# Two expert layers of a four-layer kernel: the base stored ahead of the rows, gate weights gathered apart from the rows, and half an expert's weights split per chunk in the first layer

## The chip, the cores and the metric

The kernel runs on one NeuronCore of one Trainium2 chip. The metric is the device time of one execution in microseconds; lower is better. The kernel before takes 2632.61 us, the median of 3 runs (2631.84 to 2633.73). The profile comes from one further execution, which took 2637.3 us.

The engines are called by their profile names where rows are quoted: PE (TensorE), DVE (VectorE), ACT (ScalarE), POOL (GpSimd) and SP (SyncE, which here only issues DMAs).

## The reference

The input `x` is (4, 512, 256), so T = 2048 tokens of D = 256 values, beside a context of 4 x 1601 rows. Four layers are added to `x` in turn, each fed with a layer norm of `x`:

```python
x = x + L0_xattn(ctx, layernorm(x))    # 8 heads of 128, keys from the context and x
x = x + L0_ffn(layernorm(x))           # experts, layer 0 below
x = x + L1_xattn(ctx, layernorm(x))    # 8 heads of 32
x = x + L1_ffn(layernorm(x))           # experts, layer 1 below
```

The two expert layers are what the change touches. Each has 8 experts with weights (256, 1024) and (1024, 256).

- Layer 0: scores = softmax(xn @ w_router); each token goes to its best two experts; an expert takes the first 512 of its tokens and drops the rest; h = gelu_tanh(rows @ w1); y = h @ w2; the output of a token is the sum of its score times y, plus a bias.
- Layer 1: the two largest logits (with a bias) get a softmax among themselves; h = gelu(x @ W1 + b1) with the exact gelu; out is the weighted sum of h @ W2 + b2; nothing is dropped.

## The kernel before, in words

`X` holds the 2048 tokens in SBUF as 16 tiles of 128. The function `experts` (from L940) is called once per expert layer, with `layer` 0 or 1. It has an opening and a loop over chunks of 256 rows.

**Precision.** A float32 operand is represented by two float16 numbers, a high one and a low one, and a product takes three matmuls. Expert weights come from HBM as float32 into the tile `stage` (two halves, w1 and w2, 1 MB each). `split_high` on ACT (L1176) writes the high part of a quarter of a half, `split_low` on DVE (L1183) the low part. An expert has PIECES = 8 such quarters; both functions count on semaphores (`s_wh`, `s_wl`), and SP loads a half of the next expert when the low parts of that half of the last one are written (`load_weights`, L1260).

**The opening.** PE transposes `X` and computes logits; DVE takes the statistics of the layer norm; POOL computes 1/sqrt; ACT writes the normalized rows into `xn` in two halves of eight tiles (`normalize`, L1417), splits expert 0's first half (four pieces), computes the exponential `ex` (L1435) and goes on splitting. DVE chooses the two experts of each token, and writes the gate weights `wst` (L1684, L1686). PE sums ranks (L1505 to L1511), DVE turns them into slot positions and builds one-hot matrices in `xn`'s space (L1710 to L1716), which must wait until the rows have left `xn` for HBM (L1708). PE multiplies the one-hots into the list of tokens per slot (L1535), and DVE makes `gidx` and `sidx` of it, the row indices for gathering and for scattering. In layer 1, PE also multiplies the gate weights with b2 (`pe_weighted_bias`, L1512): four before the one-hot products and four after them; ACT copies the results into `wb`.

**DMAs of the opening.** SP's queue, in order: small constants, expert 0's weights, the rows `xn` into the HBM tensor `xrow` (four parts, and in layer 1 a fifth), the gate weights into the last 8 of the 264 columns of `xrow`, expert 1's weights, then the base: `X` into the sums tensor `yd` (L1287, L1288; called `f_sums` in the rows). POOL gathers the rows of chunks 0 and 1 by an indirect DMA of 128 rows each, two per chunk, with the gate weights in the same row of 264 values (L1368 to L1372). Then it waits for the base and adds the bias (layer 0) or `wb` (layer 1) to it by four accumulating DMAs (L1393).

**The loop.** Layer 0 has 16 chunks, two per expert; layer 1 has 23, and a table that names each chunk's expert. A chunk n is turned (`pe_turn`: four transposes into `psX`; `act_turn` and `dve_turn` copy the high and low parts into `xh` and `xl`), and its 1024 hidden values are computed in 8 tiles f: `pe_hidden`, a GELU on ACT twice (L1204 to float16, L1206 to float32), the low part on DVE (L1235), `pe_output`. The turn of chunk n+1 stands inside chunk n, at f = 3 (PE) and f = 4 (ACT, DVE), and its first two hidden tiles are computed at the end of chunk n. In a chunk of the splitting loop, ACT and DVE split one piece of expert n + EARLY = n + 2 behind each f, so a whole expert's weights per chunk, until all 8 are there (`LOOPS`, L1245: three pairs of chunks with splits, the others without). In the opening, experts 0 and 1 are split, and chunk 0's first product waits until all of expert 0 is (L1545). At a chunk's end DVE multiplies the output by the gate (L1741), and POOL scatters it into the sums with two indirect accumulating DMAs (L1376). POOL's order for chunk n: gather chunk n + 2, wait for DVE, scatter chunk n. The first scatter also waits until the bias transfers have landed. The layer is over when the last scatter has landed.

## Time and profile before

| | us |
|---|---|
| median of 3 runs | 2632.61 |
| the profiled execution | 2637.3 |
| its span | 2635.5 |
| PE busy | 2417.4 (92%) |
| DVE busy | 1903.0 (72%) |
| POOL busy | 1725.7 (65%) |
| ACT busy | 1675.6 (64%) |

All stages are in one timeline, counted from the span's start. Layer 0 of the experts starts at about 1466 and ends at about 1725; layer 1 starts at about 2288 and goes to the end. A "granted clock" of 1.0 is 2.4 GHz for PE, 0.5 is 1.2 GHz. In a row of a timeline the number in brackets is the engine's idle time just before the instruction, and what ended it. Busy time of an engine counts no waiting; what an engine waits for shows in the brackets only.

### The profile page before, as it was taken

The numbers are of one execution on the slowest core, as the hardware profiler recorded it, in microseconds if no ns is written. First come the engines' busy times: TensorE is split into PE (matmuls) and PEld (weight loads), VectorE is DVE, ScalarE is ACT, GpSimd is POOL, SyncE is SP. The second block draws the span as 40 slices with busy tenths as digits, with TensorE's granted clock in tenths as the row PEclk, the third lists the DMA queues.
The fourth block names the chain that finished last, engine by engine and source line by source line (L and its number), as shares of the span: only waits on it lengthen the run. The fifth ranks groups of instructions, "written<-read, shape, count | busy, mean of one in ns | idle before, by whom it ended". The sixth has DMA issues, their size and how long they took to land. (4 is left out here: it accounts for less than half of the span.)

```text
span 2635.5 us, 45921 instructions
## 1 busy us (share of the span) xinstructions
PE 2417.4 (92%) x14931; PEld 1421.2 (54%) x15058; DVE 1903.0 (72%) x3499; ACT 1675.6 (64%) x2694; POOL 1725.7 (65%) x1503
## 2 busy tenths in 40 slices
PE   6999999999999999999998379969999999779997
PEld 3455555555555455555554268834444444458886
DVE  7878777787777877777777565448888889767443
ACT  4556756557655566655655366427888888758664
POOL 2687878687877777767678335417777779724443
PEclk9999999999999999999999589979999999869999
DMA  4000000000000000000000384241211010175323
GB/s 146 1 1 1 26 1 1 1 1 1 26 1 1 1 1 1 1 1 1 1 1 1 97 251 94 41 113 40 53 27 48 23 38 14 50 219 154 49 45 65
DMA packets 88425, 107.89 MB, mean 41 GB/s; under 512 B 16371, under 2 KB 77764, under 8 KB 88212
## 3 DMA queue, kind: packets, MB, share of 16 engines
q1 hardware_dynamic: 68500, 80.57, 10.1%
q0 software_dynamic: 19200, 24.97, 5.8%
q8 instruction: 107, 1.75, 0.3%
q14 instruction: 74, 0.60, 0.1%
q10 hardware_dynamic: 544, 0.00, 0.0%
HBM read 68.75 MB, written 25.88 MB: 36 GB/s over the span
## 5 line engine op out<-in xcount | busy, mean ns | idle before, releaser
L425 POOL TENSOR_TENSOR a_acc<-a_acc,a_pf 128x512 f32<-128x512 f32 (+1 forms) x480 | 655.3, 1365 | 309.4 <-ACT a_pf L582 287.7
L582 ACT ACTIVATE a_pf<-a_psS 128x1024 f32<-128x1024 f32 (+1 forms) x288 | 281.2, 976 | 306.4 <-PE a_psS L725 300.4
L2082 POOL TENSOR_TENSOR c_pl<-c_pf,c_ph 128x512 f16<-128x512 f32 x320 | 375.2, 1201 | 124.4 <-ACT c_ph L2181 124.0
L877 DVE TENSOR_TENSOR a_pl<-a_pf,a_ph 128x512 f16<-128x512 f32 x448 | 435.1, 981 | 23.4 <-ACT a_ph L588 23.3
L853 DVE TENSOR_REDUCE a_mx<-a_psA 128x1 f32<-128x512 f32 x504 | 337.2, 684 | 45.9 <-PE a_psA L660 40.8
L1376 POOL DMA_INDIRECT f_sums<-f_xn,f_sidx x78 | 138.0, 1770 | 235.3 <-DVE f_xn L1741 199.4
L588 ACT ACTIVATE a_ph<-a_psS 128x1024 f16<-128x1024 f32 (+1 forms) x288 | 281.0, 976 | 0.0
L2413 DVE TENSOR_REDUCE c_mx<-c_psA 128x1 f32<-128x512 f32 x384 | 246.8, 683 | 20.4 <-PE c_psA L2252 20.2
L2174 ACT ACTIVATE c_pf<-c_psS 128x1024 f32<-128x1024 f32 x192 | 197.5, 1029 | 68.9 <-PE c_psS L2286 67.6
L1235 DVE TENSOR_TENSOR f_xn<-f_xn 128x256 f16<-128x256 f32 x312 | 129.9, 424 | 134.8 <-ACT f_xn L1206 130.5
L848 DVE TENSOR_TENSOR a_vl<-a_psA,a_vh 128x256 f16<-128x256 f32 (+1 forms) x266 | 112.5, 423 | 140.8 <-ACT a_vh L511 138.1
L747 PE MATMUL a_psO<-a_pl,a_vh 128*128 128x512 f16 (+1 forms) x544 | 206.1, 379 | 7.2 <-POOL a_pl L443 7.2
L741 PE MATMUL a_psO<-a_ph,a_vh 128*128 128x512 f16 (+1 forms) x544 | 206.1, 379 | 4.0 <-DVE a_ol L882 3.9
L601 PE MATMUL a_psS<-a_qh,a_kh 128*128 128x512 f16 (+1 forms) x544 | 206.2, 379 | 0.2
L603 PE MATMUL a_psS<-a_qh,a_kl 128*128 128x512 f16 (+1 forms) x544 | 206.2, 379 | 0.0
L602 PE MATMUL a_psS<-a_ql,a_kh 128*128 128x512 f16 (+1 forms) x544 | 206.2, 379 | 0.0
L742 PE MATMUL a_psO<-a_ph,a_vl 128*128 128x512 f16 (+1 forms) x544 | 206.0, 379 | 0.0
L2181 ACT ACTIVATE c_ph<-c_psS 128x1024 f16<-128x1024 f32 x192 | 197.3, 1028 | 0.0
L660 PE MATMUL a_psA<-a_kh,a_qh 128*128 128x512 f16 x504 | 191.5, 380 | 4.2 <-DVE a_mx L853 0.4
L1135 PE MATMUL f_psH<-f_xh,f_w 128*128 128x256 f16 x624 | 172.9, 277 | 24.3 <-ACT f_xn L1206 12.7
L842 DVE SCALAR_TENSOR_TENSOR a_kl<-a_psA,a_bkv,a_kh 128x512 f16<-128x512 f32 (+1 forms) x156 | 102.8, 659 | 115.4 <-ACT a_kh L505 115.3
L1136 PE MATMUL f_psH<-f_xl,f_w 128*128 128x256 f16 x624 | 172.4, 276 | 0.0
(354 smaller groups left out, 6309.9 us busy)
## 6 DMA issues: line engine op xcount, KB each, us to landing
f_stage<-in_L_ffn_w SPq DMA_DIRECT2D x16, 1024.0 KB
f_stage<-in_L_ffn_W SPq DMA_DIRECT2D x16, 1024.0 KB, 5.6
c_kst<-c_khs SPq DMA_DIRECT2D x64, 100.1 KB, 2.2
a_cx<-in_ctx SPq DMA_DIRECT2D x4, 1536.0 KB
c_cx<-in_ctx SPq DMA_DIRECT2D x12, 512.0 KB, 3.9
f_xrow<-f_xn SPq DMA_DIRECT2D x8, 512.0 KB, 3.0
f_sums<-X SPq DMA_DIRECT2D x2, 2048.0 KB, 12.5
c_kst<-c_kls SPq DMA_DIRECT2D x32, 100.1 KB, 2.2
```

The lines of the kernel that those rows point to most:

```text
L425: g.tensor_tensor(acc[0:k, p, :], acc[0:k, p, :], pf[0:k, q % RF, i, :], ALU.add).then_inc(s_acc, 1)
L582: act.activation(pf[0:r, q % RF, 0:k, :], psS[q % 2][0:r, 0:k, :], ACT.Exp, scale=SCALE).then_inc(s_pF, 1)
L588: act.activation(ph[0:r, q % RP, 0:k, :], psS[q % 2][0:r, 0:k, :], ACT.Exp, scale=SCALE).then_inc(s_pH, 1)
L601: pe.matmul(out, hi, xh_, start=first, stop=False)
L602: pe.matmul(out, hi, xl_, start=False, stop=False)
L603: return pe.matmul(out, lo, xh_, start=False, stop=last)
L741: pe.matmul(psO[:, :], vh[0:r, g % 2, j, vs], ph[0:r, q % RP, i, :], start=(j == 0), stop=False)
L747: ins = pe.matmul(psO[:, :], vh[0:r, g % 2, j, vs], pl[0:r, q % RP, i, :], start=False, stop=(j == JT0 - 1))
L853: v.tensor_reduce(mx[:, n % 2, it, c:c + 1], ps[:, 0:KCH[c][1]], AX.X, ALU.max).then_inc(s_fr, 1)
L877: v.tensor_tensor(pl[0:r, q % RP, i, :], pf[0:r, q % RF, i, :], ph[0:r, q % RP, i, :], ALU.subtract).then_inc(s_pL, 1)
L2082: g.tensor_tensor(pl[0:r, q % RP, i, :], pf[0:r, q % RF, i, :], ph[0:r, q % RP, i, :], ALU.subtract).then_inc(s_pG, 1)
L2413: ins = v.tensor_reduce(mx[:, n % 2, it, c:c + 1], ps[:, 0:KCH[c][1]], AX.X, ALU.max)
```

## The change

Both layers:

- SP stores the base `X` into `yd` ahead of the rows and not behind expert 1's weights.
- Rows and gate weights lie in two HBM tensors, `xrow` (256 columns) and `wrow` (8 columns). POOL gathers each chunk's rows with two indirect DMAs and its weights with two more, counted on a semaphore pair of their own, `s_xw`. DVE's `dve_gate` waits for it. The store of the gate weights no longer waits for the row stores.
- ACT performs a GELU on one column, `warm`, ahead of the first turn.
- PE's first product waits for the first half of expert 0's pieces alone.

Layer 0 alone: the exponential stands between the two halves of `normalize`; POOL adds the bias to the base ahead of the first gather; expert 0's pieces have their low parts made behind the indices, all eight; expert 1 is not split in the opening. In the loop, chunk p of pair m splits half p of expert m + 1, one piece at each even f, and there is one loop over seven pairs with splits.

Layer 1 alone: one more weighted bias (of the four behind) is put between the one-hot products; the first half of expert 1 is split between the weighted biases (ACT) and behind the table (DVE), the second half behind the first turn.

The diff, cut to its core:

```diff
@@ expert weights and gate
-        s_xb, s_ys, s_bst = pool_sems
+        s_xb, s_ys, s_bst, s_xw = pool_sems
...
             for f in range(2, FT):
                 pe_hidden(pe, L, n, p, e, f)
+                if f == 2 and splits and not layer and p == 0:
+                    pe.wait_ge(s_wl, (m + 2) * PIECES)
                 pe_output(pe, L, n, p, e, f - 2)
...
-            if splits:
+            if splits and layer:
                 pe.wait_ge(s_wl, (n + 3) * PIECES)
+            elif splits and p == 1:
+                pe.wait_ge(s_wl, (m + 2) * PIECES + PH)
...
+        def split_at(m, p, f):
+            if layer:
+                return [(m * 2 + p + 2, f)]
+            return [(m + 1, p * PH + f // 2)] if f % 2 == 0 else []
...
-                if splits:
-                    split_high(act, n + EARLY, f)
+                for e, q in split_at(m, p, f) if splits else ():
+                    split_high(act, e, q)
...
-        def dve_gate(v, p, e):
+        def dve_gate(v, m, p, e):
+            v.wait_ge(s_xw[p], m * 16 * IT + 16 * IT)
+            v.nop(nofuse=True)
...
-        LOOPS = ((0, (E - EARLY) // 2, True), ((E - EARLY) // 2, PAIRS, False))
+        LOOPS = ((0, (E - 2) // 2, True), ((E - 2) // 2, PAIRS, False)) if layer else ((0, PAIRS, True),)
@@ block.sync
             for half in range(2):
                 load_weights(0, half)
+            sp.dma_start(yd[0:T, :]..., X[:, :, :]).then_inc(s_base, 16)
+            sp.dma_start(yd[T:T + CH, :]..., X[:, 0:IT, :]).then_inc(s_base, 16)
...
             sp.wait_ge(s_wst, 1)
-            sp.wait_ge(s_xst, 16 * (NQ + layer))
-            sp.dma_start(xrow[0:T, D:ROW]..., wst[:, :, :]).then_inc(s_wd, 16)
+            sp.dma_start(wrow[0:T, :]..., wst[:, :, :]).then_inc(s_wd, 16)
...
             for half in range(2):
                 load_weights(1, half)
-            sp.dma_start(yd[0:T, :]..., X[:, :, :]).then_inc(s_base, 16)
-            sp.dma_start(yd[T:T + CH, :]..., X[:, 0:IT, :]).then_inc(s_base, 16)
@@ block.gpsimd
+            def gather_weights(n):
+                for u in range(IT):
+                    g.indirect_dma_start(xb[:, n % 2, u, D:ROW], None, wrow, rows_in(n, u)).then_inc(s_xw[n % 2], 16)
...
+            if not layer:
+                g.wait_ge(s_small, 16 * NSMALL)
+                add_base(lambda q: bias[:, :].unsqueeze(1).broadcast_to([P, 4, D]))
             g.wait_ge(s_xst, 16 * (NQ + layer))
-            g.wait_ge(s_wd, 16 * (1 + layer))
             g.wait_ge(s_gidx, 1)
             gather(0)
+            g.wait_ge(s_wd, 16 * (1 + layer))
+            gather_weights(0)
             gather(1)
+            gather_weights(1)
+            if layer:
+                g.wait_ge(s_wbF, NT // 2)
+                add_base(lambda q: wb[:, 4 * q:4 * q + 4, :])
             for n in range(NC):
                 if n + 2 < NC:
...
                     gather(n + 2)
+                    gather_weights(n + 2)
@@ block.scalar
             normalize(0)
+            if not layer:
+                exponentials()
             normalize(1)
...
+                    if i == NB2 - 1:
+                        for q in range(PH):
+                            split_high(act, 1, q)
+            act.wait_ge(s_const, 3)
+            act.activation(warm[:, :], onef[:, :], GELU)
             act_turn(act, main, 0, 0)
+            if layer:
+                for q in range(PH, PIECES):
+                    split_high(act, 1, q)
@@ block.tensor
             for i in range(2 * NT):
+                if layer and i == 2 * NT - 2 * NT // NLO:
+                    pe_weighted_bias(NB2)
...
-            pe.wait_ge(s_wl, 2 * PIECES)
+            pe.wait_ge(s_wl, PIECES + PH)
             for f in range(2):
                 pe_hidden(pe, main, 0, 0, 0, f)
+            if layer:
+                pe.wait_ge(s_tab, 1)
+                pe.wait_ge(s_wl, 2 * PIECES)
@@ block.vector
-            for q in range(PH):
-                split_low(v, 0, q)
+            if layer:
+                for q in range(PH):
+                    split_low(v, 0, q)
...
-            for q in range(PH, PIECES):
+            for q in range(PH if layer else 0, PIECES):
                 split_low(v, 0, q)
...
-            for q in range(PIECES):
-                split_low(v, 1, q)
+                for q in range(PH):
+                    split_low(v, 1, q)
             dve_turn(v, main, 0, 0)
             if layer:
                 dve_bias(v, main, 0, 0, 0, wait=False)
+                for q in range(PH, PIECES):
+                    split_low(v, 1, q)
```

## Rows read from the trace of the kernel before

**Rows 1.** Busy time by stage; columns as its second line says, clock, DMA share, GB/s

```profile
1521.00:1563.00 42.00, 33.91 (x254) 26.36 (x255) 24.32 (x50) 26.54 (x66) 16.12 (x12) 0.83 0.93 246
1610.00:1725.00 115.00, 104.86 (x945) 90.54 (x943) 46.29 (x114) 53.70 (x160) 50.35 (x36) 0.99 0.28 43
```

**Rows 2.** Waits, 1520 to 1730: us in total, times, longest

```profile
POOL f_sums L1376 <- DVE f_xn L1741: 81.0, 15, 7.5
```

**Rows 3.** Timeline of the turns on ACT, layer 0: start, us, instruction

```profile
1531.24 0.66 ACT L1191 ACTIVATE f_xh<-f_psX 128x512 f16<-128x512 f32 x1
1550.07 0.60 ACT L1191 ACTIVATE f_xh<-f_psX 128x512 f16<-128x512 f32 x1
1563.02 0.60 ACT L1191 ACTIVATE f_xh<-f_psX 128x512 f16<-128x512 f32 x1
...
1610.11 0.60 ACT L1191 ACTIVATE f_xh<-f_psX 128x512 f16<-128x512 f32 x1
...
1701.80 0.60 ACT L1191 ACTIVATE f_xh<-f_psX 128x512 f16<-128x512 f32 x1
```

**Rows 4.** Timeline of the opening of layer 0, ACT and DVE

```profile
1478.09 7.95 ACT L1421 ACTIVATE f_xn<-X,f_shift,f_rstd 128x256 f32<-128x256 f32 x16
...
1488.35 0.29 DVE L1667 TENSOR_REDUCE f_sm<-f_ex 128x16 f32<-128x128 f32 x1 [5.21 <-ACT f_ex L1435]
...
1493.20 2.49 DVE L1187 SCALAR_TENSOR_TENSOR f_w<-f_stage,f_w 128x512 f16<-128x512 f32 x4
...
1498.03 1.29 DVE L1710 TENSOR_TENSOR f_xn<-f_ihi,f_hi 128x512 f16<-128x512 f16 x2
```

**Rows 5.** Windows of 2 us: us, POOL busy, PE clock, DMA share, GB/s

```profile
1522.00:1524.00 2.00, 0.00 (x0) 0.50 1.10 405
...
1530.00:1532.00 2.00, 1.39 (x3) 1.00 1.24 200
```

**Rows 6.** Timeline, chunk 0's gather and turn in layer 0

```profile
1510.52 1.22 POOL L1370 DMA_INDIRECT f_xb<-f_xrow,f_gidx  x1 [0.30 <-issue]
...
1517.55 1.11 PE L1124 MATMUL f_psX<-identf,f_xb 128*128 128x128 f32 x4 [9.82 <-DMA f_xb<-f_xrow,f_gidx]
...
1519.86 0.57 ACT L1191 ACTIVATE f_xh<-f_psX 128x512 f16<-128x512 f32 x1
```

**Rows 7.** Instruction groups, both layers: busy us, mean ns, idle before

```profile
L1204 ACT ACT_TABLE_LOAD x6 | 7.7, 1283 | 5.6 <-PE f_psH L1137 5.4
```

**Rows 8.** Timeline, waits in chunks 0 and 1 of layer 0

```profile
1527.03 0.63 ACT L1181 ACTIVATE f_w<-f_stage 128x512 f32 x1 [1.92 <-DMA f_stage<-in_L_ffn_w]
...
1541.37 0.63 ACT L1181 ACTIVATE f_w<-f_stage 128x512 f32 x1 [4.92 <-DMA f_stage<-in_L_ffn_w]
...
1547.01 1.11 PE L1124 MATMUL f_psX<-identf,f_xb 128*128 128x128 f32 x4 [3.13 <-DMA f_xb<-f_xrow,f_gidx]
```

**Rows 9.** The gathers of line 1370: ns min/median/max, first and last start

```profile
L1370 POOL DMA_INDIRECT f_xb<-f_xrow,f_gidx x78: 949/1018/1489, 1508.9 to 2592.5; - x78
```

**Rows 10.** Timeline of layer 1's opening and first chunks, PE, POOL and ACT

```profile
2326.81 7.19 PE L1516 MATMUL f_psH<-f_b,f_wt 8*128 8x256 f32 x16
...
2329.62 1.35 POOL L1370 DMA_INDIRECT f_xb<-f_xrow,f_gidx  x1 [0.30 <-ACT f_w L1445]
...
2337.19 1.09 PE L1124 MATMUL f_psX<-identf,f_xb 128*128 128x128 f32 x4 [3.19 <-DMA f_xb<-f_xrow,f_gidx]
...
2339.34 0.57 ACT L1191 ACTIVATE f_xh<-f_psX 128x512 f16<-128x512 f32 x1
...
2351.57 0.64 ACT L1191 ACTIVATE f_xh<-f_psX 128x512 f16<-128x512 f32 x1
...
2360.94 0.63 ACT L1181 ACTIVATE f_w<-f_stage 128x512 f32 x1 [3.74 <-DMA f_stage<-in_L_ffn_W]
...
2367.56 0.60 ACT L1191 ACTIVATE f_xh<-f_psX 128x512 f16<-128x512 f32 x1
...
2380.54 0.64 ACT L1191 ACTIVATE f_xh<-f_psX 128x512 f16<-128x512 f32 x1
```

More of the change, by code:

```diff
@@ L959, in experts @@
     HR = ring(FT, 3)
-    PIECES, EARLY = FT, 2
+    PIECES = FT
     PH = PIECES // 2
@@ L1732, in _ @@
                 v.sem_inc(s_tab, 1)
-            for q in range(PIECES):
-                split_low(v, 1, q)
+                for q in range(PH):
+                    split_low(v, 1, q)
             def take_rows(m, p):
@@ L2485, in build @@
                       [ctx.enter_context(nc.semaphore(f"f{l}_ys{p}")) for p in range(2)],
-                      ctx.enter_context(nc.semaphore(f"f{l}_bst"))) for l in range(2)]
+                      ctx.enter_context(nc.semaphore(f"f{l}_bst")),
+                      [ctx.enter_context(nc.semaphore(f"f{l}_xw{p}")) for p in range(2)]) for l in range(2)]
         sums = [nc.dram_tensor(f"f{l}_sums", (B * S + 2 * P, D), F32, kind="Internal").ap() for l in range(2)]
```

62 lines of the change are left out of this document (29 added, 33 removed).

## The prediction, made before the changed kernel ran

> **What bounds the kernel now.** I read the page first: the slices show TensorE at nine tenths nearly everywhere and low in two places, the openings of the two expert layers. The table of stages comes next [rows 1]: in the opening chunks of layer 0 (1521 to 1563) TensorE is busy 33.9 of 42 us at a mean granted clock of 0.83 while the DMA engines are 0.93 busy; in that layer's undisturbed part (1610 to 1725) the clock is 0.99 and the DMA engines 0.28 busy. There the table of waits [rows 2] shows GpSimd waiting for VectorE before each scatter, 81.0 us in 15 times, so 5.4 us a chunk: GpSimd has room. The timeline of the turns (the copy of a chunk's transposed rows to `xh`, one per chunk) gives the pace [rows 3]: from 1610.11 to 1701.80 eight chunks take 11.46 us each, and this is TensorE's own pace. Before it, the turn of chunk 2 comes 18.83 us after that of chunk 1, the next 12.95 us later, and the four after 47.09 us together. So a layer is a fixed pace behind a serial opening, and what the opening or its first chunks lose is lost in the end: the scatter of the last chunk ends each layer.
>
> **The change, part by part, layer 0.** *Softmax ahead.* VectorE waits 5.21 us for the exponential, until 1488.35, so its logits were ready at 1483.14; ScalarE has it behind all 16 normalizations (7.95 us from 1478.09) and four weight pieces [rows 4]. Now it stands behind eight normalizations, done at 1478.09 + 4.0 = 1482.1, so it starts at about 1483.3: VectorE resumes 4.75 us earlier. *Four low splits out of the chain.* 2.49 us of VectorE [rows 4] leave the stretch between the gate weights and the slot positions; part of them covered TensorE's rank products, so I count 1 us. The one-hots, from 1498.03, could start at 1492.3. *Base stored first.* They also wait until the normalized rows have left `xn`. The 2.36 MB of base now go into the row stores' queue in front of them. At the 405 GB/s of [rows 5] they need 5.8 us, begin when the first weights are in (about 1475.6) and are out by about 1482. The accumulating bias transfer follows at once, where the DMA engines are 1.24 busy and move only 200 GB/s [rows 5], so it takes some 10 to 12 us, from about 1484, beside the second half of the row stores (1.6 us per 512 KB alone, twice that when shared), the last of which is now issued at 1487.5, since the exponential and the later normalizations move it by 1.4 us. I put their landing at 1494.5: the one-hots gain 3.5 us, not 5.7. Bounds: no sharing, 5.7; the rows behind the whole accumulation (about 1500), a loss of 2. *Gather.* The second half of chunk 0's rows is issued by 1511.74 and TensorE starts on them at 1517.55 [rows 6], 5.8 us later, with a weight load and the base beside them. Now the base is gone and the weight loads start after the gather. Bounds: 5.8 again, or 2 us. I take 3.0, near the low end because the gather's neighbours leave: gain 2.8. *Splits behind the turn.* Four weight pieces on ScalarE kept the turn at 1519.86 [rows 6], though the four transposes ended 1.11 us after 1517.55: 1.2 us gained, since expert 1 is not split in the opening any more. Opening: 3.5 + 2.8 + 1.2 = 7.5 us.
>
> The Trainium skill ("DMA: Bandwidth & Descriptors", Anatomy of one DMA) fits a software-made DMA as 2.0 us plus bytes over 436e3, so 2.3 us for half a chunk's rows; by that estimate the gather would gain 3.5 us instead of my 2.8, and the measured 5.8 us is what crowded engines make of it.
>
> *First chunks of layer 0.* Six table loads of 1.283 us each stand before a GELU [rows 7]: in both layers at the first GELU and at the head of the first loop's two later rounds. The `warm` GELU makes one of each three, hidden in the wait for the gather, and leaves the loop none: the second loop, which is entered from a GELU, shows none today. ScalarE also waits 1.92 us for a stage in chunk 0 and 4.92 us in chunk 1, and TensorE 3.13 us for the rows of chunk 2 [rows 8]. Both have one cause, the crowd on the DMA engines: base, bias and weights two experts ahead, all after 1511. In the new kernel base and bias are done at about 1497, chunk 0 needs only the first half of expert 1, and chunk 1 the second. So chunk 2's turn comes 11.46 us after chunk 1's instead of 18.83: 7.4 us (the fallen clock after the stall is in this number). The next gains 12.95 - 11.46 = 1.5. The four to 1610.11 lose 47.09 - 45.84 = 1.25, a table load and a change of loops; I take 1.0. Chunk 0's own first interval, 11.38 us, holds a table load and the 1.92; TensorE's work at half clock stands right behind them, so of 3.2 I take 2.0. *Half an expert a chunk.* 56 splits in the loop instead of 48, four a chunk to the last pair. The chunks with eight splits keep the pace apart from those 1.25 us, and ScalarE has 53.7 of 115 us busy in the unsplit part [rows 1], so four (2.5 us) are nearly free; I charge 0.1 us for each of eight more chunks, 0.8. Layer 0: 7.5 + 2.0 + 7.4 + 1.5 + 1.0 - 0.8 = 18.6 us.
>
> *Weights gathered apart*, both layers. Two more indirect DMAs a chunk on GpSimd. No row has a gather of 32 bytes a row; the nearest is the row gather, median 1.02 us [rows 9] and 0.30 us to the next instruction, so 2.6 us a chunk, out of 5.4 us of waiting [rows 2]: nothing. In the opening they push gather(1) back by 2.6 us, needed only at the fourth tile of chunk 0, about 7 us after the first turn. VectorE's new wait for them stands behind the low half of the turn, and ahead of the first `hl`, 4 us later; they land before. Bounds: nothing, and with 5 us a pair the excess over the cover, which is a rival below.
>
> **Layer 1.** *One weighted bias between one-hot products.* Four of them take 7.19 us [rows 10], one 1.8. It goes into a gap of 0.7 us, in which TensorE waits for the last one-hots, so the slot indices come 1.1 us later. *Gather and turn.* Issued by 2330.97, rows used at 2337.19 [rows 10], 6.2 us later; with the base gone but a weight load beside it I take 4.1 (bounds 2 and 6.2): 2.1 gained. The turn at 2339.34 waited behind four splits, psX being ready at 2338.28: 1.0. So 2.0 in all. *First chunks.* Interval of the turns 12.23 us, then 15.99, then 12.98 [rows 10]. The first has a table load and a wait for a stage, as in layer 0: 2.0 gained. The second holds ScalarE's 3.74 us wait for a stage [rows 10] and one for rows. Here the accumulation cannot start before the weighted biases and four more gathers (about 2340, 4 us earlier than now), and expert weights still go two ahead: the crowd is only thinned by the base's 6 us. Bounds 0 and 4.3; I take the middle, 2.4. The third gains most of its table load, 0.8, and a later one 0.4. Layer 1: 2.0 + 2.0 + 2.4 + 0.8 + 0.4 = 7.6 us. Base before the row stores costs nothing there: weights, base and rows are 6.8 MB, 17 us at 405 GB/s from the stage's start at about 2291, so out by some 2312 with the gaps; the one-hots that wait for them are built in the ten us before 2326.81.
>
> **Sum.** 18.6 + 7.6 = 26.2 us. The profiled execution has 2637.3 us (span 2635.5 and 1.8 around it) and gives 2611.1; the median, 2632.6, gives 2606.4. I forecast 2606.5.
>
> ScalarE's page of the Trainium skill ("ScalarE: Activation LUTs", What ACT_TABLE_LOAD costs) adds a drain of about 1.38 us to each load, so 2.66 us. Six loads, two of them left and hidden, would by that return up to 16 us in place of the 5 or so that I have for them in the terms above. The rows do not bear it out: four chunks with one load and a change of loops in them lose 1.25 us in all against the pace [rows 3].
>
> **Rivals.** *A, the row stores are caught behind the accumulation* in layer 0. For it: both start within a few us, and accumulation halves the rate [rows 5]. Against: the stores of three quarters are issued before it is under way. Where the rows land only at 1500, the 3.5 turn into -2: 2606.5 + 5.5 = 2612. *B, layer 1 gains only its opening and tables*, since its crowd is merely moved: without 2.4 and half of the first interval's 2.0, 2606.5 + 3.4 = 2610; with the gathers of both layers no faster (2.8 + 2.1) it is 2615. For it: [rows 10] show weights late with hardly any base left in the queue. *C, the openings clear out completely*: no sharing of the row stores (2.2), layer 1's second interval at its best (1.9), gathers at 2 us (1.0 + 2.1): 2606.5 - 7.2 = 2599. *D, GpSimd becomes the bound*: two weight gathers a chunk cost more than the 5.4 us of cover. It decides from 2.7 us for each. At 3.5 us each, seen nowhere in the trace (longest gather 1.49 [rows 9]), it is 1.6 us over in each of 37 chunks, 59 us, less the 26 gained: 2640, slower. *E, the change does not do what it says*: table loads stay in the loops because the compiler places them anew; 3 us less gain, 2609.5.
>
> **How the numbers follow.** Forecast 0.45, A 0.15, B 0.17, C 0.13, D 0.03, E 0.07. The range takes in C and both forms of B: 2599 to 2617. What a measurement can tell from no change is 0.2%, 5.3 us. Faster than that: all but D and a rest in which several bad ends meet, 0.95; within it 0.02; slower 0.03.
>
> **What would show it.** The exponential of layer 0 at about 1483 and one-hots from 1492 to 1497, with VectorE waiting for the row stores if I am right on sharing; turns of chunk 0 near 1512 and 2337; three turns in layer 0 at 11.5 us from the second on, without a clock at half; one table load a layer, ahead of the first turn; GpSimd's wait before scatters at 2.7 us. The forecast is wrong if a chunk's pace in the later part of either layer moves by more than 0.2 us (rival D or dearer splits), if one-hots start after 1498, or if layer 1 still has a 16 us interval.

## The result, and the profile after

| | before | after |
|---|---|---|
| median, us | 2632.23 (2631.44 to 2633.73, 4 runs) | 2617.27 (2615.52 to 2619.40, 4 runs) |
| the profiled execution, us | 2637.3 | 2615.5 |

The ratio is 0.9944, 95% interval 0.993 to 0.9959: 15 us faster, where 26 were forecast. A later comparison on another chip (`after_control` below) has 0.9955 (0.9941 to 0.9968), 10.6 us. The time lies just outside the range, above its upper end of 2617.

Layer 0's opening is where the forecast and the chip part first. The timelines of ScalarE, VectorE, GpSimd, SyncE and TensorE in the kernel after (columns as in [rows 3] and [rows 4]):

```profile
1483.44 0.31 ACT L1455 ACTIVATE f_ex<-f_sh 128x128 f32<-128x128 f32 x1 [1.12 <-DVEq L1702]
...
1492.20 0.19 DVE L1749 TENSOR_TENSOR f_hi<-f_pos,f_lo 128x32 f16<-128x32 f32 x1
1499.94 1.29 DVE L1752 TENSOR_TENSOR f_xn<-f_ihi,f_hi 128x512 f16<-128x512 f16 x2 [7.55 <-DMA f_xrow<-f_xn]
...
1483.36 5.52 POOL L1396 DMA_DIRECT2D f_sums<-f_bias  x4 [2.89 <-DMA f_sums<-X]
1510.72 1.26 POOL L1387 DMA_INDIRECT f_xb<-f_xrow,f_gidx  x1 [21.84 <-DVE f_gidx L1760]
1512.29 1.38 POOL L1387 DMA_INDIRECT f_xb<-f_xrow,f_gidx  x1 [0.30 <-issue]
...
1480.38 7.68 SPq L1294 DMA_DIRECT2D f_xrow<-f_xn  x4
1512.83 2.78 SPq L1284 DMA_DIRECT2D f_stage<-in_L_ffn_w  x2
...
1518.11 1.11 PE L1126 MATMUL f_psX<-identf,f_xb 128*128 128x128 f32 x4 [8.49 <-DMA f_xb<-f_xrow,f_gidx]
```

The exponential stands at 1483.44, as forecast, and VectorE has the slot positions at 1492.39. Then it waits 7.55 us for the row stores out of `xn`: the one-hots start at 1499.94, 1.9 us after those of [rows 4], and not 3.5 us before. SyncE issues the four row stores at 1480.38, 1482.35, 1485.74 and 1487.70; GpSimd issues the four accumulations of the bias from 1483.36 to 1488.88, so three of them go out ahead of the third row store. The last row store, from issue to landing, in the kernel after, and then in `e1_again` (below), where no accumulation runs beside it (count, KB, us to landing):

```profile
f_xrow<-f_xn SPq DMA_DIRECT2D x1, 512.0 KB, 12.1
```

```profile
f_xrow<-f_xn SPq DMA_DIRECT2D x1, 512.0 KB, 3.1
```

The windows of that stretch in the kernel after (POOL busy, clock, DMA share, GB/s):

```profile
1486.00:1488.00 2.00, 2.00 (x3) 0.50 1.09 151
...
1492.00:1494.00 2.00, 0.00 (x0) 0.50 1.20 210
...
1496.00:1498.00 2.00, 0.00 (x0) 0.50 1.24 226
1498.00:1500.00 2.00, 0.00 (x0) 0.50 1.46 201
1500.00:1502.00 2.00, 0.00 (x0) 0.50 0.88 85
```

The packets' times add up to more than the 16 engines have (a share over 1), and in these windows the engines move 151 to 226 GB/s, near the 200 GB/s of the accumulation in [rows 5], until about 1501. The last accumulation has landed at 1502.7. The turns of layer 0 after that, and two turns from its later part:

```profile
1528.58 0.60 ACT L1204 ACTIVATE f_xh<-f_psX 128x512 f16<-128x512 f32 x1
1539.88 0.60 ACT L1204 ACTIVATE f_xh<-f_psX 128x512 f16<-128x512 f32 x1
1551.66 0.60 ACT L1204 ACTIVATE f_xh<-f_psX 128x512 f16<-128x512 f32 x1
...
1608.99 0.60 ACT L1204 ACTIVATE f_xh<-f_psX 128x512 f16<-128x512 f32 x1
...
1689.21 0.60 ACT L1204 ACTIVATE f_xh<-f_psX 128x512 f16<-128x512 f32 x1
```

The first turn is at 1519.26 (before: 1519.86), and then 9.32 and 11.30 us follow where [rows 3, 6] had 11.38 and 18.83. The windows that answer [rows 1], and GpSimd's wait that answers [rows 2]:

```profile
1519.00:1561.00 42.00, 39.68 (x338) 33.49 (x337) 24.82 (x55) 27.16 (x74) 23.82 (x20) 0.93 0.48 126
...
POOL f_sums L1401 <- DVE f_xn L1783: 47.5, 16, 8.9
```

TensorE has 39.7 of 42 us busy (33.9 before), the DMA engines 0.48 (0.93). GpSimd's wait ahead of the scatters is 47.5 us in 16, 3 us a chunk, and still a wait: the two weight gathers a chunk, 0.94 us each, are covered. The pace is unmoved: 11.46 us a chunk from 1608.99 to 1689.21 (seven chunks), as in [rows 3].

Layer 1's turns, GpSimd's stretch behind them, and TensorE's wait for chunk 2's rows:

```profile
2320.98 0.60 ACT L1204 ACTIVATE f_xh<-f_psX 128x512 f16<-128x512 f32 x1 [2.57 <-PE f_psX L1126]
2330.68 0.60 ACT L1204 ACTIVATE f_xh<-f_psX 128x512 f16<-128x512 f32 x1
2347.51 0.60 ACT L1204 ACTIVATE f_xh<-f_psX 128x512 f16<-128x512 f32 x1
2360.20 0.60 ACT L1204 ACTIVATE f_xh<-f_psX 128x512 f16<-128x512 f32 x1
...
2322.86 5.38 POOL L1396 DMA_DIRECT2D f_sums<-f_w  x4
2328.54 1.11 POOL L1387 DMA_INDIRECT f_xb<-f_xrow,f_gidx  x1 [0.30 <-issue]
2344.39 1.71 POOL L1401 DMA_INDIRECT f_sums<-f_xn,f_sidx  x1 [10.57 <-DMA f_sums<-f_w]
...
2345.35 0.65 PE L1126 MATMUL f_psX<-identf,f_xb 128*128 128x128 f32 x4 [2.52 <-DMA f_xb<-f_xrow,f_gidx]
```

The second interval, chunk 1's, is 16.83 us, against 15.99 in [rows 10] and 13.6 forecast.

A stage that the change doesn't touch also moved: from the last turn of layer 0 to layer 1's exponential it is 607.2 us before and 603.1 after. The windows of that attention stage, before and after (columns as in [rows 1]):

```profile
1725.05:2288.62 563.57, 518.35 (x2716) 258.51 (x2716) 465.76 (x823) 435.79 (x516) 405.30 (x367) 0.96 0.16 41
```

```profile
1712.46:2271.59 559.13, 512.74 (x2716) 256.71 (x2716) 465.02 (x823) 435.65 (x516) 405.04 (x367) 0.98 0.16 41
```

The same 2716 products, granted 0.96 and 0.98. Over all 21 traces this stretch, from turn to exponential, lies between 602.9 and 608.1 us with no relation to the edits, so its 4.1 us (4.4 between the edges of these windows) are not put down to the change. Stages are therefore compared below from marks inside them.

### The profile page after: what moved, and what is told of

The parts are those of the page before. It is cut to its first block and busy times, and to the rows that moved or that the text cites. A ratio compares the mean times of both kernels' runs of the same rounds, so it can differ in the third digit from the quotient of the medians.

```text
span 2613.7 us, 46134 instructions
## 1 busy us (share of the span) xinstructions
PE 2408.0 (92%) x14931; PEld 1418.7 (54%) x15058; DVE 1906.1 (73%) x3499; ACT 1673.0 (64%) x2692; POOL 1806.8 (69%) x1581
## 5 line engine op out<-in xcount | busy, mean ns | idle before, releaser
L877 DVE TENSOR_TENSOR a_pl<-a_pf,a_ph 128x512 f16<-128x512 f32 x448 | 437.1, 985 | 23.4 <-ACT a_ph L588 23.3
L2457 DVE TENSOR_REDUCE c_mx<-c_psA 128x1 f32<-128x512 f32 x384 | 246.7, 683 | 19.9 <-PE c_psA L2296 19.7
```

What stands on the lines that cost most here:

```text
L877: v.tensor_tensor(pl[0:r, q % RP, i, :], pf[0:r, q % RF, i, :], ph[0:r, q % RP, i, :], ALU.subtract).then_inc(s_pL, 1)
L2457: ins = v.tensor_reduce(mx[:, n % 2, it, c:c + 1], ps[:, 0:KCH[c][1]], AX.X, ALU.max)
```

## The experiments

Marks: N is the start of layer 0's normalization, X the exponential of layer 1, T0, T1, ... the turns (in the text N to T0 means the time between them). All columns are us; "time" is the median of the kernel's runs (one run where it stands in brackets), "pace" is one chunk between T8 and T15 of layer 0. Six of them ran at a slower pace, as the last column shows (see below).

| kernel | time | N to one-hots | N to T0 | T0 to T2, layer 0 | X to T0 | T0 to T2, layer 1 | pace |
|---|---|---|---|---|---|---|---|
| before | 2632.2 | 19.9 | 41.8 | 30.2 | 30.3 | 28.2 | 11.5 |
| c1_before_again | 2629.1 | 19.9 | 41.9 | 30.2 | 30.2 | 27.9 | 11.4 |
| after | 2617.3 | 21.6 | 41.0 | 20.6 | 28.7 | 26.5 | 11.5 |
| after_control | 2618.7 | 20.9 | 40.3 | 21.0 | 29.0 | 26.7 | 11.5 |
| c0_after_again | 2682.9 | 21.6 | 41.1 | 20.2 | 29.1 | 26.1 | 13.4 |
| e1_bias_after_rows | 2674.0 | 14.4 | 31.5 | 22.6 | 28.8 | 26.3 | 13.8 |
| e1_again | 2608.7 | 14.3 | 31.5 | 20.1 | 28.9 | 26.6 | 11.5 |
| e1_third | 2607.4 | 14.4 | 31.5 | 20.3 | 28.9 | 26.5 | 11.5 |
| e2_stage_held | (2621.0) | 20.7 | 37.5 | 21.2 | 28.9 | 27.8 | 11.5 |
| v2 | 2609.3 | 14.3 | 30.5 | 21.2 | 28.9 | 27.4 | 11.5 |
| e5_no_warm_gelu | (2615.2) | 20.7 | 40.3 | 20.3 | 28.9 | 26.2 | 11.5 |
| e6_base_back | (2697.5) | 14.1 | 33.6 | 31.6 | 29.6 | 29.2 | 13.9 |
| e6_again | (2626.4) | 14.1 | 33.5 | 31.8 | 29.5 | 29.4 | 11.5 |
| e8 | (2620.4) | 20.4 | 39.8 | 26.0 | 28.7 | 26.0 | 11.4 |
| e9 | (2619.9) | 21.2 | 40.5 | 21.3 | 28.1 | 27.5 | 11.5 |
| e3_gather2_first | (2691.6) | 20.9 | 40.6 | 20.7 | 29.0 | 24.0 | 13.5 |
| e4_l1_no_accum | (2684.9) | 22.0 | 41.4 | 20.7 | 28.9 | 23.3 | 13.8 |
| e4_again | (2612.3) | 20.5 | 39.9 | 21.0 | 28.9 | 22.1 | 11.5 |
| v1 | 2690.1 | 24.0 | 43.4 | 21.1 | 33.4 | 28.5 | 13.7 |
| v3 | 2606.1 | 14.4 | 31.2 | 20.8 | 26.0 | 25.3 | 11.5 |

The kernels whose opening of layer 0 is that of the kernel after have one-hots 20.4 to 22.0 us behind N: a difference under 2 us there says little, and against the 19.9 of before they lose 0.5 to 2.1.

**The bias accumulated behind the rows (e1).** Rival A, put to the test:

```diff
-            if not layer:
-                g.wait_ge(s_small, 16 * NSMALL)
-                add_base(...bias...)
             g.wait_ge(s_xst, 16 * (NQ + layer))
+            if not layer:
+                g.wait_ge(s_small, 16 * NSMALL)
+                add_base(...bias...)
```

> The changed kernel with one move in layer 0: the accumulating bias transfers are issued only when the row stores have landed. Main theory: the one-hots of layer 0 waited 7.55 us for the rows (until 1499.94) because the accumulation ran beside the row stores. Then they start at 1492.5 to 1494 here, the turn of chunk 0 moves from 1519.3 to 1512 to 1514, and the time falls by 5.5 to 7 us (about 2611). Rival: the rows are late because they stand behind the 2.36 MB of base in the same queue. Then the one-hots start no earlier than 1498 and the time stays within 2 us.

The one-hots start 14.4 us behind N and the first turn 31.5, 9.5 us earlier than in the kernel after, so the theory held and its 5.5 to 7 us were too few. The base still stands in front of the row stores here, which rules out the rival. The total went the other way, 2674.04 us (2672.93 to 2678.09), because its loops ran at another pace; see the control below. Repeated beside a copy of the kernel after:

> Layer 0's four accumulations of the bias are issued behind the wait for the rows' stores, and not in front of them. In one look their one-hot matrices started 14.35 us behind the start of the normalization against 21.6 in the kernel after, and the first turn came 31.5 us behind it against 41.0; the third turn 8.3 to 9.1 us earlier. Theory: 8 to 9 us faster than the kernel after beside it, and 2607 to 2610 where that takes 2617: the forecast gain of layer 0's opening was to be had. Rival: the accumulations, now landing beside the first gather, cost it again in chunks 0 to 2, and it gains 0 to 4 us.

Measured 2608.68 (2604.73 to 2611.27, 5 runs), ratio to before 0.9918 (0.9904 to 0.9931), against 2618.70 (2614.43 to 2619.19) for `after_control`: 10 us faster by moving one wait over four DMAs. The opening of `e1_again`:

```profile
1491.05 5.53 POOL L1396 DMA_DIRECT2D f_sums<-f_bias  x4 [10.65 <-DMA f_xrow<-f_xn]
1502.78 1.11 POOL L1387 DMA_INDIRECT f_xb<-f_xrow,f_gidx  x1 [6.20 <-DVE f_gidx L1760]
...
1492.57 1.29 DVE L1752 TENSOR_TENSOR f_xn<-f_ihi,f_hi 128x512 f16<-128x512 f16 x2
...
1509.73 0.60 ACT L1204 ACTIVATE f_xh<-f_psX 128x512 f16<-128x512 f32 x1 [16.46 <-PE f_psX L1126]
1518.56 0.60 ACT L1204 ACTIVATE f_xh<-f_psX 128x512 f16<-128x512 f32 x1
```

The row stores have landed by 1491.05, VectorE waits for nothing, and the accumulation runs while VectorE builds the one-hots. Against `after_control` the accumulation in front costs 6.6 us of one-hots and 8.8 of the first turn; from N to the last turn of layer 0 it is 201.0 us for 210.7.

**Two paces of one program.** On the chip of the first e1 ran also e3, e4 and e6. e3 moves layer 1's accumulation behind chunk 2's gather:

```diff
-            if layer: ... add_base(...wb...)
             for n in range(NC):
                 if n + 2 < NC: ... gather(n + 2); gather_weights(n + 2)
+                if layer and n == 0: ... add_base(...wb...)
```

> The changed kernel with one move in layer 1: the gathers of chunk 2 are issued ahead of the accumulating transfers. Theory a: the 16.8 us interval of the turns of chunks 1 and 2 has 2.5 us of waiting for rows because the gather stands in GpSimd's queue behind the accumulation (plus the fall of the clock, if any, after it). Then the interval is 13.5 to 14.5 us. Theory b: it is the bandwidth that the accumulation takes, whatever the order. Then the gather's wait shrinks little, or comes back one chunk later, since the first scatter waits for the accumulation: the sum of the two intervals (29.5 us) stays within 1 us.

e4 leaves that accumulation out, so its output lacks the term with b2:

```diff
                 g.wait_ge(s_wbF, NT // 2)
-                add_base(lambda q: wb[:, 4 * q:4 * q + 4, :])
+                g.wait_ge(s_base, 32)
...
-                    g.wait_ge(s_bst, 16 * NQ)
+                    if not layer:
+                        g.wait_ge(s_bst, 16 * NQ)
```

> The changed kernel without the accumulating transfers of layer 1 (the weighted bias b2 is left out of the sums; all else is computed). Theory a (the accumulation is what crowds chunk 1): the intervals of the turns, 16.8 and 12.7 us, become 11.5 to 12.3 and 11.7; layer 1 loses 5 to 6 us. Theory b (expert weights two experts ahead are enough of a crowd by themselves): ScalarE's waits for a stage, 2.1 and 0.9 us in chunks 0 and 1, remain and the first interval stays above 13.5 us.

e6 puts the base's stores back, and with them layer 0's bias accumulations behind the gathers of chunks 0 and 1 (the diff shows the first part):

```diff
-            sp.dma_start(yd[0:T, :]..., X[:, :, :]).then_inc(s_base, 16)
-            sp.dma_start(yd[T:T + CH, :]..., X[:, 0:IT, :]).then_inc(s_base, 16)
...
             for half in range(2):
                 load_weights(1, half)
+            sp.dma_start(yd[0:T, :]..., X[:, :, :]).then_inc(s_base, 16)
+            sp.dma_start(yd[T:T + CH, :]..., X[:, 0:IT, :]).then_inc(s_base, 16)
```

> The changed kernel with the base stored behind expert 1's weights again, and layer 0's bias added behind the gathers of chunks 0 and 1, as before; the rest of the change stays. Main theory: layer 0's one-hots no longer wait for the rows (start 1492.5 to 1493.5, gain 7 us), but the crowd of base, bias and weights is back in the first chunks: the gather lands 1 to 2 us later than in the changed kernel, and chunks 1 and 2 lose 3 to 8 us; in layer 1 the interval of chunks 1 and 2 stays at 16 us or more. Rival: with half an expert a chunk the crowd no longer matters in layer 0, and the intervals stay at 11.3 to 11.8 us: then this version is faster than the changed kernel by 6 us or more.

And the kernel after, with no edit:

> The changed kernel, unchanged, run again beside the others. Four variants of it, whose PE instructions are the same, took 2674 to 2697 us, with a pace of 13.7 us a chunk in layer 0 where the changed kernel had 11.5, and PE 'issue' waits of 20 us in a stretch of 100. If the slow pace belongs to the variants' own edits, this one repeats 2617 us. If it belongs to a property of the program's loading or of the run (where the loop's instructions lie, how they are fetched), this one may show 2670 us or more too, though nothing in it differs.

All six programs on these two chips (v1 below is the sixth) took 2674 to 2697 us, and `c0_after_again`, which is the kernel after to the last instruction, 2682.87 (2681.77 to 2683.97). The kernel before, beside them, kept its time (2631.96 and 2633.24). Its loop, ScalarE from 1610 and the weight loads' waits from 1600 to 1700 (us in total, times, longest), then the same waits in the first trace of the kernel after:

```profile
1612.29 0.41 ACT L1219 ACTIVATE f_xn<-f_psH 128x256 f32<-128x256 f32 x1
1614.83 0.38 ACT L1217 ACTIVATE f_xn<-f_psH 128x256 f16<-128x256 f32 x1 [2.13 <-PE f_psH L1139]
...
PEld f_psH L1137 <- issue: 19.7, 19, 2.0
```

```profile
PEld f_psH L1137 <- issue: 2.3, 4, 0.7
```

Engines stop in turn for 1 to 2 us behind nothing that the profile shows. It isn't TensorE's clock: the window of 1600 to 1700 (PE busy, clock, DMA share, GB/s) of `c0_after_again`, then of the kernel after, has the clock at 1.00 in both and the DMA engines equally busy.

```profile
1600.00:1700.00 100.00, 85.47 (x748) 1.00 0.48 113
```

```profile
1600.00:1700.00 100.00, 97.61 (x876) 1.00 0.47 106
```

Layer 0 takes 27 us more from its first to its last turn (197.3 for 170.4), layer 1 36 more from X to its last turn (324.7 for 289.0). The marks ahead of the loops differ far less: those of `c0_after_again` lie within 0.8 us of `after_control`, those of the first e4 within 1.6 us of `e4_again`, and T0 to T2 of the first e1 (22.6) is 2.5 us off. So the openings can be read, for effects well above that.

> The kernel before, unchanged, placed beside itself as the other experiments are, since the kernel after took 2683 us so placed against 2617 when it was first measured, with its expert loops at 13.7 us a chunk against 11.5. Theory 1: any program placed as the experiments are pays this in its expert loops; then this copy takes about 2690 to 2700 us against 2632 of the same instructions beside it, with turns of layer 0 in the loop 13 to 14.7 us apart instead of 11.3 to 12.1. Theory 2: only the change's loops can fall into the slower pace; then it takes 2632 and its turns stand 11.3 and 12.1 apart.

2629.06 (2626.93 to 2631.14), beside 2629.46 for the kernel before: unmoved. But this doesn't decide between the theories, since the kernels beside it, and all that ran later on two more chips, had the normal pace, among them e1, e4, e6 and the kernel after, unchanged:

> The kernel after, unchanged, as the control beside the next three. On two chips a copy took 2683 us with its expert loops at 13.7 us a chunk; on the chip of the first measurement 2617, and three near-copies on another chip took 2615, 2620 and 2621. If the slower pace belongs to some chips or loads, this copy and its three neighbours stand at the same pace, whichever it is; if it belongs to single programs, they differ from each other.

Kernels of the new form on one chip agreed each time, so the pace goes with the chip or the occasion and not with the edit, and the kernel before has never shown it. What it is stays open.

**The stage loads held (e2, v2).** SyncE waits for chunk 0's rows before it loads expert 1:

```diff
+            if not layer:
+                sp.wait_ge(main.xb[0], 16 * IT)
             for half in range(2):
                 load_weights(1, half)
```

> SyncE's two stage loads of expert 1 in layer 0 (1 MB each) wait until chunk 0's rows are gathered. In the kernel after, the gather's second issue ended at 1513.67 and TensorE's first transpose of its rows started at 1518.11: 4.4 us where 3.0 were predicted; the stage loads are issued from 1512.83 and fill all queues from 1515. Theory (the gather's packets stand behind the stage loads'): without them the gather lands 2.5 to 3.2 us after its issue, the first turn is 1.2 to 1.9 us earlier, and chunk 0's splits of expert 1 start 3 to 4 us later, so that the third turn gains nothing. Rival (the landing is the gather's own): 4.4 us as before, the first turn unmoved and the next two later. The total isn't decisive at this size; the turns are.

The second gather issue ended at 1513.23 and TensorE had the rows 1.8 us later:

```profile
1515.07 1.11 PE L1126 MATMUL f_psX<-identf,f_xb 128*128 128x128 f32 x4 [5.89 <-DMA f_xb<-f_xrow,f_gidx]
```

1.8 for 4.4 us: the loads had stood in the gather's way. The first turn comes 2.9 us earlier (1.2 to 1.9 expected) and the third 2.7, 58.7 us behind N for 61.4 in `after_control`, where no gain was expected. No gain shows in the total of the one run, 2620.98, with 2 us of it in the untouched stage and 2.6 more in layer 1.

> As e1_again, and SyncE's two stage loads of expert 1 in layer 0 wait until chunk 0's rows are gathered. The hold by itself brought the first turn 3.0 us forward and the third 2.4 us; in the one look at the later bias the gather landed 2.85 us behind its issue without a hold, against 4.4. Theory 1 (both waits are of the same queue, and the later bias has already moved the stage loads off the gather): as e1_again within 1 us, or up to 1 us slower, since the stage loads come later. Theory 2 (they add up): 2 to 3 us faster than e1_again.

2609.28 (2604.69 to 2611.49), as e1: theory 1. The gather landed in 1.85 us against 2.86, and the first turn is 1.0 us earlier, which the next interval gives back, 9.9 for 8.8. TensorE's mean granted clock in that interval is 0.70 for 0.74; over the kernels at the normal pace (the kernel before and e8 apart) it is 8.8 to 10.1 us long, so a difference of 1 us there is not put down to an edit.

**The table loads (e5).**

```diff
-            act.wait_ge(s_const, 3)
-            act.activation(warm[:, :], onef[:, :], GELU)
```

> Leaves out ScalarE's warm-up activation behind the softmax, so the table load for the activation function falls behind the first turn again, in both layers. Theory of the prediction (a table load of 1.28 us is on the path only if it stands behind the turn): the first turn of either layer is unmoved within 0.3 us, and the interval from the first to the second turn grows by 1.0 to 1.3 us in each layer against the kernel after placed alike (9.76 and 9.29 us there). Rival: ScalarE waits there for the hidden products anyway (the wait of 2.4 us ahead of the first of them), and the intervals stay.

2615.24, and intervals of 8.99 and 9.89 us where `after_control` has 9.74 and 10.10. The loads are back:

```profile
L1217 ACT ACT_TABLE_LOAD x10 | 12.8, 1283 | 6.5 <-PE f_psH L1139 6.4
```

Ten for two, and nothing lost in one run (2615.24 lies within the runs of the kernel after). The rival held, though not by the wait that it named: the first load of layer 0 stands behind the wait of 2.36 us and delays the GELU by its 1.29 us, and it is the next waits for hidden products, 0.62, 0.75 and 1.10 us in `after_control`, that take it up. That the interval is even shorter goes with a mean granted clock of 0.77 for 0.66. The Trainium skill ("ScalarE: Activation LUTs", What ACT_TABLE_LOAD costs) has 2.66 us for each switch, a drain included; eight more of them would be 21 us by it. This run shows none of that in the total, and no drain beside this load: the GELU starts at 1523.65, 1.29 us after it.

**The order of the splits (e8) and of the base (e6).** The core of e8's edit (the loop bounds and TensorE's waits go back with it, and expert 1 is split behind the first turn):

```diff
-            return [(m + 1, p * PH + f // 2)] if f % 2 == 0 else []
+            return [(m * 2 + p + 2, f)]
```

> Undoes the order of the splits in layer 0 alone: every chunk of the loop splits a whole expert's weights, two ahead, as in the kernel before (10 splits of high and low parts ahead of the loop, 8 a chunk in it), all else as in the kernel after. Theory (the half-expert order took 2.0 us off the first interval and 7.4 off the second, which stood for the second expert's stage loads): the intervals behind the first turn, 9.8 and 10.5 us in the kernel after placed alike, go to 11 to 12 and 16 to 19 us. Rival (the long second interval of before was made by TensorE's clock, at 1.2 GHz until 1547, and the loads landing late behind the base's store, which is gone here too): 10 to 11.5 and 11 to 13.5.

14.56 and 11.39 us, 2620.40 in all. Both missed the first interval, and only the rival has the second: the wait for the second expert's load falls in chunk 0 (3.94 us), not in chunk 1, and the two together lose 4.9 us; at the third turn 4.4 of them are left (65.8 behind N for 61.4). For the base, at the normal pace:

> The base's two stores (2.25 MB) go back behind the stage loads of expert 1 on SyncE's queue, in both layers, and layer 0's bias accumulations behind chunk 1's gathers; the rest as in the kernel after. In a look at the slower pace layer 0's first turn came 33.6 us behind the start of the normalization (41.0 in the kernel after) and the second interval was 21.6 us. Theory (the store beside the stage loads makes the long second interval, as in the kernel before with its 18.8): first turn at 33 to 35 us behind the normalization, second interval 17 to 21, the third turn within 1 us of the kernel after. Rival (the 21.6 was of the slower pace): 13 or less.

Turn at 33.5 as expected, intervals 8.85 and 22.92, longer than expected, and the third turn 3.9 us behind the kernel after, where 1 us at most was expected; 2626.41 in all, in one run. The third turn of layer 0 sorts the parts (us behind N): 72.1 in `c1_before_again`, 65.2 in e6, 61.4 in `after_control`, 51.6 in e1. So all the rest of the change is worth 6.9 us there (the one-hots alone are 5.8 us earlier), and the base in front with the bias behind it brings only 3.9 more, because the delay of the one-hots takes back most of what the chunks gain; with the accumulation moved behind the row stores it brings 13.6. In layer 1 it brings 3.2 us as made (58.9 from X to the third turn for 55.7). e6 moves base and accumulation together, so their shares in the long interval of 22.92 us are not separated.

**Layer 1: the accumulation (e4, e3), and one weighted bias (e9).**

> Leaves out layer 1's accumulation of the weighted bias (the term with b2 is then missing from the output), all else as in the kernel after. In one look at the slower pace the first three intervals of layer 1 were 11.39, 11.88 and 13.77 us against 9.29, 16.81 and 13.23. Theory (the accumulation in front of chunk 2's gather makes the 16.8): the second interval falls to 11 to 12.5 us, and the three together from 39.2 us to 33.5 to 35.5. Rival (the stage loads alone make the second interval): 15 or more.

Second interval 11.91 us instead of 16.60; the next is the same, 12.75. The three are 34.9 us for 39.4, and X to the last turn is 284.3 for 289.0. At the slower pace, `e3_gather2_first` (the accumulation behind chunk 2's gather) had 12.60 in place of 16.81 but then 23.37 for 13.23, both of its expectations missed and 8 us worse in the end: GpSimd waits 17.99 us for the accumulation ahead of its first scatter, and chunk 3's gather stands behind that scatter. In `v1_sums_on_gpsimd` GpSimd adds bias and base itself and stores the sums, in place of SyncE's store and the accumulation:

```diff
+                g.tensor_tensor(wb[:, ts, :], X[:, ts, :], plus, ALU.add).then_inc(s_pool, 1)
+                g.wait_ge(s_pool, q + 3)
+                g.dma_start(yd[4 * q * P:(4 * q + 4) * P, :]..., wb[:, ts, :]).then_inc(s_bst, 16)
```

> The changed kernel without the base store and without the accumulating transfers: GpSimd adds the bias (layer 0) or the weighted bias (layer 1) to X in SBUF (four additions of 128x1024) and stores the sums with plain DMAs. If the accumulation is the cause of both losses (row stores late in layer 0, the crowd in layer 1), the one-hots of layer 0 start at 1492 to 1495, the turn of chunk 0 comes near 1513, and layer 1's interval of 16.8 us becomes about 12; 10 to 12 us less than the changed kernel at the same pace of the loops. If bandwidth of the weight loads is the cause in layer 1, its interval stays above 14.

Row stores no longer share with an accumulation, and VectorE waits for none of them, and yet the one-hots come 24.0 us behind N. VectorE's timeline says why:

```profile
1481.97 2.05 DVE L1710 TENSOR_TENSOR f_lg<-f_eq,f_rstdw 128x128 f32<-128x128 f32 x1
1484.06 0.29 DVE L1714 TENSOR_REDUCE f_m<-f_lg 128x16 f32<-128x128 f32 x1
1484.38 3.40 DVE L1715 TENSOR_TENSOR f_sh<-f_lg,f_m 128x128 f32<-128x128 f32 x1
```

Two additions of GpSimd, 2.3 us each, end at 1483.88 and 1487.62; VectorE's two instructions that meet them, of 0.29 us elsewhere, take 2.05 and 3.40 us and end 0.15 us behind. The other two additions stretch two more, to 2.44 and 3.09 us: 9.8 us in all four. The Trainium skill ("SBUF — State Buffer", SBUF: two separate sides) has the cause: the two engines lock one port pair for a whole instruction, and the other waits it out. The trace agrees, but for one point: by the page the one that starts first gets the pair, and VectorE's 3.40 us are on record from 1484.38, 0.9 us ahead of the addition that it waits out (GpSimd is issuing a DMA then). So GpSimd's room is no room for additions of this size beside VectorE's chain. In layer 1 the second interval is 11.88 us, as the theory had it, but the first turn comes 4.3 us later and the first interval is 16.6 us. 2690.12 us, 7 slower than `c0_after_again` beside it.

e9 takes the inserted weighted bias out from between the one-hot products:

```diff
-                if layer and i == 2 * NT - 2 * NT // NLO:
-                    pe_weighted_bias(NB2)
...
-                for i in range(NB2 + 1, NT // 2):
+                for i in range(NB2, NT // 2):
```

> Layer 1's fifth pair of weighted-bias products goes back behind the one-hot products, all else as in the kernel after. Theory of the prediction (it takes 1.1 to 2.0 us out of the stretch behind the one-hot products, ahead of the first turn): first turn of layer 1 up to 2 us later, measured from the start of its exponential (29.0 us in the control). Rival (the turn waits for the gather, not for TensorE): unmoved, within 0.3 us.

X to T0 is 28.1 us and not 29.0: the inserted product costs 0.9 of the first turn. It was charged with 1.1 in the prediction; this expectation had forgotten the sign. At the third turn nothing is left of it (55.6 us behind X for 55.7).

**Half of layer 1's accumulation earlier (v3).** As e1, and in layer 1 the accumulation of the first two quarters goes into the idle stretch ahead of the indices:

```diff
             g.wait_ge(s_xst, 16 * (NQ + layer))
...
+            else:
+                for q in range(NQ // 2):
+                    g.wait_ge(s_wbF, 2 * q + 2)
+                    add_base(lambda q: wb[:, 4 * q:4 * q + 4, :], [q])
```

> As e1_again in layer 0; in layer 1 the accumulations of the weighted bias of the first two quarters of the rows (1 MB) are issued as soon as these quarters are computed, at about 2297 and 2300, where the queues lie idle until 2308 (DMA share 0.06 and 0.02 in the windows from 2294 and 2298), and the other two where all four stood. Theory (the accumulation costs 4.7 us in chunks 1 and 2 by the time it holds chunk 2's gather, about evenly by quarter): the second interval falls from 17.0 to 14 to 15 us, the first turn moves by no more than 0.5, and the kernel is 2 to 3 us faster than e1. Rival (the early halves delay the gather of chunk 0, or the two late ones cost as much as four): first turn 1 to 3 us later or interval still 16 or more, and no gain.

> The same kernel as e1_again, as the control beside v3_two_quarters_early: 2609 us, second interval of layer 1 17.0 us.

2606.13 (2603.31 to 2607.68), ratio to before 0.9914 (0.9900 to 0.9929), beside 2607.35 (2606.19 to 2608.67) for e1. The medians are 1.2 us apart, and the ranges overlap, so the 2 to 3 us are not shown by time. The trace has more: X to T0 26.0 us for 28.9, second interval 14.98 for 17.16, third turn 4.1 us earlier from X and the last 4.4. The two accumulations, and the queues while they run:

```profile
2293.98 1.45 POOL L1396 DMA_DIRECT2D f_sums<-f_w  x1 [17.27 <-ACT f_w L1479]
2295.69 1.30 POOL L1396 DMA_DIRECT2D f_sums<-f_w  x1 [0.26 <-ACT f_w L1479]
```

```profile
2296.00:2300.00 4.00, 0.99 (x1) 0.50 1.19 154
2300.00:2304.00 4.00, 0.49 (x1) 0.50 0.73 114
```

The second has landed at 2303.67, when the gather is issued (2303.51). That the first turn gained 2.9 us wasn't expected. The gather's last issue ends 1.2 us earlier behind X than in e1; and the stage load is issued at 2306.28, behind that end (2305.94), and TensorE starts on the rows 3.2 us after it (released by ScalarE, the rows were there) instead of 5.1. I read the second part as the hold of e2, come about by itself; that is argued, and a hold in layer 1 wasn't tried.

## Why the prediction was wrong, by its steps

- **Base stored first, layer 0's one-hots: the step that failed.** It let the one-hots gain 3.5 us, with the rows landed at 1494.5; they landed at 1499.9 and the one-hots lost 1.9. The mechanism, the halved rate of [rows 5] over the row stores, was named, and rival A gave its end, 1500 and -2. What failed is the price of the overlap: a 512 KB store was put at twice its 1.6 us beside the accumulation, and the last one took 12.1 us from issue to landing (3.1 in e1); the accumulation was put at 10 to 12 us and took 19.3 (15.1 in e1, with no row store beside it). The argument against A was false as well: two quarters' stores, not three, are issued ahead of the accumulation, and it is the last store that frees `xn`. e1 shows that the whole 5.6 us, and the turn's 10, were there.
- **Gather, 2.8 us.** 5.8 became 4.4, not 3.0: "the weight loads start after the gather" was false by 0.8 us. With a hold it is 1.8. This and the one-hots make the opening's 0.6 us for 7.5 (1.6 in the later pair, `c1_before_again` against `after_control`).
- **Softmax ahead, splits behind the turn.** VectorE resumed at 1483.78, 4.57 us earlier (4.75). The transposes' end and the turn fell together, as said.
- **First chunks of layer 0.** 2.06 and 7.53 us for 2.0 and 7.4, right in size. That the first of them fits is in part luck: the table loads, in which the terms 2.0, 1.0, 0.8 and 0.4 had a part, are worth nothing (e5). Undone one at a time, the base's move costs 3.9 us at the third turn (e6) and the order of the splits 4.4 (e8). From T2 to the last turn it was 2.4 us for 1.7, but only 0.4 in the later pair.
- **Half an expert a chunk, weights gathered apart.** The pace is 11.46 before and after; 0.94 us for a gather of weights. Rival D is out. Its price in the prediction was a wrong sum besides: 59 us less the 26 gained, on 2632.6, is 2666 and not 2640.
- **Layer 1, 7.6 us.** 5.4 in the two profiles from X to the last turn, but 1.1 between `c1_before_again` (290.0) and `after_control` (289.0). The opening gave 1.6 us for 2.0 (1.2 in the later pair). The second interval, "the middle" of 0 and 4.3, lost 0.8 (1.7 in the later pair): the accumulation starts 4.6 us earlier from X, as said, but it still stands in front of chunk 2's gather and still takes 4.7 (e4). Rival B in essence, though B counted the tables, which gave nothing.
- **Sum.** Layer 0 12.8 for 18.6, layer 1 5.4 for 7.6; in the later pair 11.2 and 1.1. The profiled execution of before was 4.7 us over its median, and 3.8 of its layer 1 don't recur in its copy: taking gains from it and subtracting them from the median kept gains that belonged to that trace.

A and B together give 2606.5 + 5.5 + 3.4 = 2615.4; I had priced them one at a time and given both 0.32. Two of the three signs of being wrong came true: one-hots after 1498, and an interval of 16 us in layer 1.

## What to carry to other kernels

In these runs a DMA that accumulates held the plain transfers beside it, so it belongs where nothing that gates an engine is still under way: here behind the stores that free a buffer (10 us by time), and in an idle stretch of the queues (4.4 us by trace). When a transfer is moved forward, follow its neighbour to its landing, not its issue. Before sizing terms of 1 to 4 us from one profile, hold it against a second one of the same kernel.

## What the runs showed of the hardware

- One program had two paces, 2617 and 2683 us, its loops 11.5 or 13.4 us a chunk (near-copies up to 13.9), with "issue" waits of the weight loads of 2.3 or 19.7 us in 100 and the granted clock at 1.00 in both; the cause is open.
- Four accumulations of 512 KB took 15.1 us from first issue to last landing (`e1_again`, no row store beside them), and beside two row stores 19.3. A 512 KB row store issued at 1487.70 landed 12.1 us later beside them, 3.1 us later without them.
- A chunk's gathered rows (two DMAs of 128 KB) took 1.8 us from the end of the last issue to use with the stage loads held, 2.9 with the first of them issued 0.2 us before the gather's end, and 4.4 with 0.8 us.
- A table load delayed the activation behind it by 1.29 us, and eight more of them cost nothing that shows in the total.
- Additions of 2.35 us on GpSimd stretched four VectorE instructions of 0.29 us to 2.05 to 3.40 us.
- A stage that no edit touches took 602.9 to 608.1 us.
